# More dense edge blocks, narrower tiles and a shorter k/v cycle in a graph block's kernel

## The reference

```
deg_out = segment_sum(w, src);  deg_in = segment_sum(w, dst)
norm = w * rsqrt(deg_out[src] * deg_in[dst] + eps)
h6 = relu(segment_sum((xn @ W6)[src] * norm, dst) + b6)
h7 = relu(segment_sum((h6 @ W7)[src] * norm, dst) + b7)
gnn = h7 @ Wp + bp
k, v = layernorm of each head of xn @ wk.T, xn @ wv.T   (4 heads of 64)
mix = (q @ (k.T @ v / N)) @ wo.T + bo
x = x + gnn + mix
x = x + layernorm(mixture of 2 of 8 experts(layernorm(x)) + layernorm(x))
```

## Time and profile before

| | |
|---|---|
| time, median of 3 runs | 3923.15 us (3919.55 to 3930.97) |
| span of the profiled execution | 3561.3 us |
| that execution's own time | not given apart from its span; 361.9 us lie between span and median |
| TensorE busy in the span | 2813.0 us (79%) |
| GpSimd | 2357.1 us (66%) |
| VectorE | 1936.5 us (54%) |
| ScalarE | 950.0 us (27%) |
| indirect DMAs (line 1908) | 2040 of 1002 ns, idle before them 684.0 us, of which 604.2 us issue |
| pass 1, first to last gather starts | 449.2 to 1910.2 us |
| pass 2 | 1933.3 to 3154.5 us |

### The profile page before, as it was taken

One profiled execution on the slowest core, in us unless ns is written; L12 is line 12 of the kernel. 1 busy time (PEld: TensorE's weight loads), 2 busy tenths in 40 slices (PEclk: granted clock), 3 DMA queues, 4 the chain that ended last, 5 costly groups with the idle time before them and its releaser, 6 DMA issues.

```text
span 3561.3 us, 51404 instructions
## 1 busy us (share of the span) xinstructions
PE 2813.0 (79%) x15774; PEld 1830.9 (51%) x15774; DVE 1936.5 (54%) x5283; ACT 950.0 (27%) x3210; POOL 2357.1 (66%) x2283
## 2 busy tenths in 40 slices
PE   4565558998989889998953577888778868869998
PEld 4454425555556555655521345555546535545666
DVE  9999846787778777877752142222243242232334
ACT  6787642332333323332220020000020010012111
POOL 5776577777777777777765777777777777730000
PEclk8788979999999999999975799999989999989999
DMA  4110035555555555555555546566646646642221
GB/s 132 59 44 1 2 104 151 167 159 151 162 164 158 150 157 170 155 156 160 166 177 156 170 149 195 197 201 200 195 147 196 197 153 193 198 156 95 79 71 49
DMA packets 260757, 511.33 MB, mean 144 GB/s; under 512 B 64843, under 2 KB 138459, under 8 KB 260141
## 3 DMA queue, kind: packets, MB, share of 16 engines
q0 software_dynamic: 97920, 268.62, 26.0%
q1 hardware_dynamic: 156057, 232.90, 19.7%
q10 hardware_dynamic: 6500, 6.40, 0.5%
HBM read 398.63 MB, written 109.15 MB: 143 GB/s over the span
## 4 chain that ended last, share of the span: by engine, by line
POOL 32%; PE 25%; DVE 15%; issue 12%; DMA 10%; SPq 4%; DVEq 1%; ACT 1%; ACTq 0%; POOLq 0%
POOL ringb L1908 31%; PE ps L676 7%; DVE ab L1058 6%; PE ps L845 5%; PE ps L858 5%; DMA ringb<-t,src 4%; PE ps L653 3%; DVE ab L1056 3%; DMA ab<-in_x 2%; SPq L1969 2%; PE ps L637 2%; SPq L1964 1%; DMA ab<-ad 1%; DMA rsd_in<-rdi 1%; POOL ab L1881 1%
## 5 line engine op out<-in xcount | busy, mean ns | idle before, releaser
L1908 POOL DMA_INDIRECT ringb<-t,src x2040 | 2044.2, 1002 | 684.0 <-issue 604.2
L676 PE MATMUL ps<-xb,ab 125*128 125x256 f32 (+1 forms) x4100 | 1062.0, 399 | 23.0 <-DMA ab<-ad 20.9
L676 PEld LDWEIGHTS ps<-xb,ab 125*128 125x128 f32 x4100 | 796.6, 199 | 287.1 <-issue 103.1
L653 PE MATMUL ps<-mlb 128*125 128x350 f32 x1176 | 495.6, 512 | 127.8 <-DVE mlb L1250 82.5
L637 PE MATMUL ps<-ringb,Sb 128*32 128x257 f32 (+1 forms) x4080 | 348.8, 416 | 280.6 <-DMA ringb<-t,src 178.2
L1697 ACT ACTIVATE ab<-ps 125x300 f32 x637 | 284.3, 446 | 671.0 <-PE ps L653 617.1
L559 PE MATMUL ps<-ab 128*50 128x125 f32 x3240 | 245.9, 306 | 183.3 <-ACT ab L1624 127.6
L1881 POOL TENSOR_TENSOR ab<-ab,wn 128x100 f32<-128x100 f32 x202 | 276.4, 1374 | 126.4 <-DVE ab L1056 126.4
L653 PEld LDWEIGHTS ps<-mlb 128*125 128x125 f32 x1176 | 208.6, 201 | 281.7 <-DVE mlb L1250 163.7
L637 PEld LDWEIGHTS ps<-ringb,Sb 128*32 128x32 f32 x4080 | 83.3, 111 | 496.7 <-DMA ringb<-t,src 273.7
L559 PEld LDWEIGHTS ps<-ab 128*50 128x50 f32 x3240 | 207.8, 143 | 221.2 <-DVE ab L1058 189.2
(11 more groups left out here) (231 smaller groups left out, 2520.8 us busy)
## 6 DMA issues: line engine op xcount, KB each, us to landing
ad<-ab SPq DMA_DIRECT2D x200, 312.5 KB
ab<-ad SPq DMA_DIRECT2D x200, 312.5 KB
ringb<-t,src POOLq DMA_INDIRECT x2040
x2t<-mlb SPq DMA_DIRECT2D x13, 500.0 KB, 18.5
xb<-x2t SPq DMA_DIRECT2D x13, 500.0 KB, 8.2
xb<-in_x SPq DMA_DIRECT2D x10, 625.0 KB
t<-xb SPq DMA_DIRECT2D x10, 625.0 KB
kvb<-t SPq DMA_DIRECT2D x50, 125.0 KB
```

The lines of the kernel that those rows point to most:

```text
L653: e.matmul(PS[(2, 7, 4, 5)[bank_of(t)]][0:R, 0:HR], low[:, slot_of(t), :], high[:, slot_of(t), :], start=True, stop=True).then_inc(s_bld, 1)
L676: ins = e.matmul(PS[3][:, 0:wd], lhs, X[0:R, k, 0:wd], start=k == 0, stop=k == NT - 1)
L1908: e.indirect_dma_start(msg[:, slot * QT + k, 0:width], None, table, bass.IndirectOffsetOnAxis(src[:, t:t + 1], 0)).then_inc(s_g[slot], 16)
```

## The change

- ND = 21 dense chunks instead of 18, one every PD = 11 steps instead of 13. Pass 1 has 246 steps, pass 2 has 216. Pass 1 builds 630 tiles (588 before), 2 or 3 a step, and makes 1050 dense matmuls (900); pass 2 makes 1300 (1150).
- NY = 5 instead of 3: all five extra chunks are built in pass 2, over YB = 6 steps each, four tiles a step; 120 tiles instead of 72. The groups are others (GX).
- RT = 6 node columns a dense tile instead of 7, so a build has 300 columns instead of 350.
- `Lb` is compared for all tiles of a step in one VectorE instruction, and multiplied by the weight on ScalarE, one instruction a tile (`weigh_lo`), between the first and the second eviction of the step before.
- The k and v weights are centred once on each head ahead of pass 1, and k/v tiles take KV = 4 steps in place of 5, without the mean and the subtraction.
- The degree row becomes the third part of the ring, 128 partitions wide, so that one VectorE add, memset or merge covers all three; the degree's transposes have 128 equal stationary columns instead of one.
- ScalarE scales five node tiles a step at the start of pass 1 instead of four.

```
-ND = 18
+ND = 21
-NY = 3
-YB = 8
-GX = [17, 44, 7, 26, 35]
+NY = 5
+YB = 6
+GX = [4, 11, 18, 30, 35]
-PD = 13
-RT = 7
+PD = 11
+RT = 6
+KV = 4
...
+        acc3 = accb[:, :].rearrange("p (h n) -> p h n", h=3)
...
-                    e.matmul(bank[0:1, 2 * P:3 * P], ag[:, D:D + 1], ident[:, :], start=True, stop=True)
+                    e.matmul(bank[:, 2 * P:3 * P], ag[:, D:D + 1].to_broadcast([P, P]), ident[:, :], start=True, stop=True)
...
+            heads = wkv.rearrange("p h (a d) -> p (h a) d", d=64)
+            e.tensor_reduce(means, heads, AX.X, ALU.add).then_inc(s_cen, 1)
+            e.tensor_scalar(means, means, 1.0 / 64, None, ALU.mult).then_inc(s_cen, 1)
+            e.tensor_tensor(heads, heads, means.unsqueeze(2).to_broadcast([P, 16, 64]), ALU.subtract).then_inc(s_cen, 1)
...
-                    e.tensor_reduce(h8[0:R, 0, :], ps3, AX.X, ALU.add).then_inc(s_kv, 1)
-                    e.tensor_scalar(h8[0:R, 0, :], h8[0:R, 0, :], 1.0 / 64, None, ALU.mult).then_inc(s_kv, 1)
-                    e.tensor_tensor(kk, ps3, h8[0:R, 0, :].unsqueeze(2).to_broadcast([R, 8, 64]),
-                                    ALU.subtract).then_inc(s_kv, 1)
...
-                    o = acc[:, :, bass.ds(b, W)]
-                    if L == 0:
-                        o = degr[:, bass.ds(b, W)]
-                        e.tensor_tensor(o, o, bank[0:1, 2 * P + j * W:2 * P + (j + 1) * W], ALU.add).then_inc(s_dad, 1)
+                    o = (acc if L else acc3)[:, :, bass.ds(b, W)]
...
-                for k in range(n):
-                    e.tensor_scalar(Lb[:, o + k, :], iof[:, 0:R], srcf[:, c0 + k:c0 + k + 1], wn[:, c0 + k:c0 + k + 1],
-                                    ALU.is_equal, ALU.mult).then_inc(s_L, 1)
+                e.tensor_tensor(Lb[:, o:o + n, :], iof[:, 0:R].unsqueeze(1).to_broadcast([P, n, R]),
+                                srcf[:, c0:c0 + n].unsqueeze(2).to_broadcast([P, n, R]), ALU.is_equal).then_inc(s_lo, 1)
...
+            def weigh_lo(s):
+                b = BUILD_AT[0].get(s)
+                if not b:
+                    return
+                e.wait_ge(s_lo, batches_before(s) + 1)
+                for k, t in enumerate(b):
+                    row = Lb[:, s % 2 * MLS + k, :]
+                    e.activation(row, row, ACT.Copy, scale=wn[:, TS + t:TS + t + 1]).then_inc(s_L, 1)
...
-                    for t in BUILD_AT[0].get(s, ()):
+                    for t in BUILD_AT[0].get(s, ())[:1]:
+                        evict(t)
+                    weigh_lo(s + 1)
+                    for t in BUILD_AT[0].get(s, ())[1:]:
                         evict(t)
```

More of the change, by code:

```diff
@@ L192 @@
 STEPS0 = max(max(HID_AT) + 2, LAST + 1)
-KV_STEPS = NT * 5
+KV_STEPS = NT * KV
 LATE_AT = FIRST + max(KV_STEPS + 2, DY * PD - 4)
@@ L433, in gnn_block @@
         s_g = [sem(f"s_g{i}") for i in range(RQ)]
[L434 to L437, removed]
+        s_eq, s_S, s_mm, s_cp, s_tr, s_add, s_pass = (
+            sem(k) for k in ("s_eq", "s_S", "s_mm", "s_cp", "s_tr", "s_add", "s_pass"))
+        s_xs, s_M, s_lo, s_L, s_az, s_bld, s_ev, s_c0, s_r0, s_mul, s_lc, s_tc = (
+            sem(k) for k in ("s_xs", "s_M", "s_lo", "s_L", "s_az", "s_bld", "s_ev", "s_c0", "s_r0", "s_mul", "s_lc", "s_tc"))
         l_as = [sem("l_as0"), sem("l_as1")]
@@ L683, in dense_turn @@
                 if L == 0:
-                    e.matmul(bank[0:1, 2 * P:3 * P], agd[:, D:D + 1], ident[:, :], start=True, stop=True)
+                    e.matmul(bank[:, 2 * P:3 * P], agd[:, D:D + 1].to_broadcast([P, P]), ident[:, :], start=True, stop=True)
                 for h in range(2):
@@ L1132, in merge @@
                 m = merged[0]
[L1133 to L1134 removed]
+                merged[0] += 2
+                spill = acc3[:, :, CR:CR + SP_]
                 e.wait_ge(s_add, added[0])
[L1136 to L1138 removed]
+                e.tensor_tensor(acc3[:, :, 0:SP_], acc3[:, :, 0:SP_], spill, ALU.add).then_inc(s_mrg, 1)
+                e.wait_ge(s_mrg, m + 1)
+                e.memset(spill, 0.0).then_inc(s_mrg, 1)
                 e.wait_ge(s_mrg, m + 2)
[L1140 to L1142 removed]
             merged, added, freed = [0], [0], [1]
@@ L1212, in add @@
             def add(L, g):
-                bank = PS[g % 2]
+                bank, n = PS[g % 2], 2 if L else 3
                 for j in range(QT):
@@ L1231, in add_chunk @@
                 e.wait_ge(s_tc, L * ND + d + 1)
-                o = acc[:, :, bass.ds(b, P)]
-                e.tensor_tensor(o, o, PS[3][:, 0:2 * P].rearrange("p (h c) -> p h c", h=2),
-                                ALU.add).then_inc(s_add, 1)
-                if L == 0:
-                    if added[0]:
-                        e.wait_ge(s_dad, added[0])
-                    o = degr[:, bass.ds(b, P)]
-                    e.tensor_tensor(o, o, PS[3][0:1, 2 * P:3 * P], ALU.add).then_inc(s_dad, 1)
+                o, n = (acc if L else acc3)[:, :, bass.ds(b, P)], 2 if L else 3
+                e.tensor_tensor(o, o, PS[3][:, 0:n * P].rearrange("p (h c) -> p h c", h=n), ALU.add).then_inc(s_add, 1)
                 added[0] += 1
@@ L1712, in scale_rows @@
             def scale_rows(s):
-                for t in range(4 * s, min(4 * s + 4, NT)):
+                for t in range(5 * s, min(5 * s + 5, NT)):
                     if t == 0:
```

71 lines of the change are left out of this document (31 added, 40 removed).

## The result

The changed kernel takes 3766.45 us (3763.83 to 3778.75, four runs), the kernel before 3924.47 us (3919.55 to 3930.97, four runs) beside it: a ratio of 0.9614 [0.9595, 0.9632], 158 us faster. 3748 was forecast.

What follows compares the result with a forecast made beforehand. Gathers pace the kernel before; after the change TensorE bounds pass 1. Pass 1's last gather 88 us earlier and pass 2 in 1119 us give span 3386, 175 under 3561.3; 3923 - 175 = 3748 us, range 3690 to 3810.

Steps and rivals of the forecast that it cites:

- the forecast's own signs: Gathers 984 and 864; pass 1 step 5.6 to 5.9 us, TensorE over 92%; pass 2 step 5.1 to 5.3.
- rival B: Pass 1 paced by the chain through ScalarE's weighing: 6.2 us a step, +99 us, 3846 us; chance 0.18.
- C: Pass 1, same weighing chain with VectorE's adds never overlapping it: 7.0 us a step, +274 us, 4021 us; chance 0.06.
- The span and the 362 us: Whole run: 362 us of the 3923 us median lie outside the profiled span of 3561.3 us and stay unchanged.
- What bounds before: Both passes before the change: GpSimd's gathers set the pace, 5.38 and 5.09 us a step, TensorE a close second in pass 1.
- The step of pass 1: Pass 1 body: TensorE becomes the bound, 5.38 us of work plus 0.37 us of waits, 5.75 us a step.
- The weighing: ScalarE in pass 1: 0.36 us an instruction, a chain of about 4.7 us, uncovered only at chunk changes, within the 0.37 us.
- Port: Pass 1 gathers: without VectorE's tensor_scalars the pitch falls from 1.345 towards 1.25 us; the sum does not move.
- Pass 2: Pass 2: TensorE's work 4.81 us against gathers at 5.0; 5.18 us a step, 216 steps in 1119 us.
- rival D: Pass 2 held by TensorE and the stored chunks' loads: 5.6 us a step, +91 us, 3838 us; chance 0.09.
- the loads of stored chunks are covered: Pass 2: ten pieces of a stored chunk are issued in 25.4 us, and a chunk lasts 35 us.
- Turn and end: Turn to pass 2 grows from 23.1 to 26 us; after the last gather, 9 us more output stream and 5 us TensorE lag.

Runs made afterwards that it cites:

- the two bodies with work left out: Compares first, against the kernel before on the fast chip: a tenth of the stored blocks' traffic, 3346.41 us; three gathers a step instead of four, 3438.61 us.
- the run with work left out: Compares first and 20 of each chunk's 50 dense matmuls in pass 1 left out, against the kernel before on the fast chip: 3459.62 us, ratio 0.9711.
- the run with work added: Compares first and seven node columns a dense tile instead of six, against the kernel before on the fast chip: 3559.44 us, ratio 0.9993.

## Why the prediction was right, and where it was not

The time was right, 3748 for 3766, and each piece of the table of stages came within 17 us. The reasons hold only in part, and a good part of the hit is luck: a difference worked out on the fast chip's rows met one of nearly the same size on a slow chip, where other things make it up. Of the forecast's own signs only the gather counts (984 and 864) came there. The step was 6.50 us and not 5.6 to 5.9, TensorE 85% busy and not over 92%, the gathers' pitch before step 12 was 1.45 us and not near 1.25, pass 2 took 5.98 us a step and not 5.1 to 5.3. A step over 6.1 us was to mean rivals B or C, with TensorE waiting for the weighed one-hots; the trace gives that wait 7.4 us in 1200.

- **The span and the 362 us.** Wrong. "362 us of the 3923 median lie outside it, and I leave them alone": they were the difference of two chips, nearly all of it in the two passes (174 and 166 us). The forecast took a difference worked out at one pace and applied it at another.
- **What bounds before.** Right for the profile read, wrong for the executions timed. There the step of 6.07 us was never the gathers'; 24 fewer steps saved some 24 x 6.07 = 146 us, and the others got longer, so that 72 us were left.
- **The step of pass 1.** +0.37 us forecast over the old 5.38; +0.43 measured on the slow chip (6.07 to 6.50). The pitches of the parts stand in the trace after (a build 0.51 us for 0.506, a dense matmul 0.435):

```profile
1126.35 1.03 PE L678 MATMUL ps<-xb,ab 125*128 125x257 f32 x4
1127.22 0.67 PE L656 MATMUL ps<-mlb 128*125 128x300 f32 x2
1127.73 1.90 PE L678 MATMUL ps<-xb,ab 125*128 125x257 f32 x8
```

The fast chip's bodies bear out "TensorE becomes the bound" there: 5.54 us a step with a quarter of the gathers gone, 5.39 with the 20 matmuls gone. The 5.75 us was not measured there, as the changed kernel wasn't; with six columns the two bodies with work left out took 5.53 and 5.54, with seven it is 5.80. On the slow chips it fails: leaving out 183 us of its work gave 35. What paces them is the round trip in part (38 us came back when the compares were put first); the rest, late results and the lower clock, has no shown cause.

- **The weighing.** The instruction was taken at 0.36 us and is 0.394 us (630 of them). That its chain is "covered in steps with dense work, uncovered at the chunk change", and paid for by the 0.37, was too light. Of rival B the mechanism is shown: the weighing costs 17 us where it stands, 51 us at the end of the step, nothing once the compares come first. Its size, +99 us, was not reached by it.
- **Port.** Wrong. The gather's pitch was to fall towards 1.25 us in pass 1. The long gather it read ended at 1008.28 us, 0.05 us ahead of the last tensor_scalar's 1008.33 and not after it. The gathers' mean in the body of the fast chip is 928.52 / 892 = 1.041 us with the tensor_scalars and 908.59 / 872 = 1.042 us without them, and the line at 1114.23 above shows a gather of 1.63 us that ends only after two tensor_tensors. The forecast leaned on one sentence of the Trainium skill, "SBUF — State Buffer", section "Who interferes with whom", and passed over another there: a VectorE instruction with two inputs in SBUF contends with a GpSimd instruction that reads SBUF. The new compares have two inputs in SBUF; by that sentence the long gathers stay if an indirect gather's reading of its row numbers counts, and the trace agrees with it; that this reading is the reason no run here shows. As the forecast said, this did not move its sum.
- **Pass 2.** 5.18 us a step was forecast, from 5.09. On the slow chip it went from 5.79 to 5.98, on the fast one from 5.09 to 5.66. There the rule "the loads of stored chunks are covered" failed and rival D (5.6 us by the loads) is what happened; it had been given 0.09. On the slow chip the dense matmuls of the changed kernel waited only 3.9 us for loads in the whole pass, and the gain of 96.5 us came because the old pass was itself slow: 24 steps of 5.79 are 139 us, less 216 x 0.20.
- **The small edits.** The forecast has no sum for them alone. Measured without the blocks they are next to nothing: 1.0031 with the weighing on ScalarE, 0.9988 without.
- **Turn and end.** +7.6 and +10.4 for +3 and +14.

So the same arithmetic on the chip of the profile would have missed. With the compares first and six columns the change lies there between the run with work left out and the run with work added, 3459.6 to 3559.4 us (if less work is never slower): a gain of 2 to 102 us, where the forecast's own rows gave 175. The exact gain of the change there was not measured.

## What to carry to other kernels

Compare the span of a profile with the times before anything is added to or taken from it: a gap of 362 us is not overhead until a second profile says so. Where several engines pass one-hots, products and sums round in a circle, price the circle in the order of each engine's queue, not by the busy shares; here moving one call past some adds gave 38 us, and taking 183 us off the busiest engine 35. Look at the granted clock before and after, too: part of the work taken off TensorE came back as a slower clock. When gathers are traded for stored blocks, the loads of the blocks can take the gathers' place as what the pass waits for, as they did on the fast chip.

## What the runs showed of the hardware

- One program ran in 3918, 3921 and 3562 us on three chips, each within 0.6% over 13 runs, with equal median lengths of its instructions. The mean granted clock of the whole runs was 0.873, 0.873 and 0.905. What makes TensorE's results late on the slower chips, and what lowers the clock there, stays open.
- In these two paces TensorE's time at the upper clock level is nearly the same (2895 and 2860 us of the program); the slower run has 999 us at the lower level for 682.
- A gather issued by GpSimd takes 0.95 us in the median. In the body of pass 1 on the fast chip 125 of 891 took over 1.2 us (up to 2.03) before the change and 121 of 872 (up to 1.89) with the compares as tensor_tensors and the 20 matmuls left out; 107 of the 125 and 98 of the 121 overlap one of VectorE's two large compares, against 291 of the 766 and 254 of the 751 shorter ones.
- Gathers slow the loads of stored blocks: with a quarter of the gathers left out the dense matmuls of pass 2 waited 88.0 us for loads instead of 128.0.
- A ScalarE multiplication by a column on 128 x 125 elements takes 0.394 us on the mean, a copy out of PSUM of 125 x 250 elements 0.405 us.
